# Attention and mixture-of-experts layer on one core: maximum ahead of the preceding weighted sum, other unit order, norm in portions, column sums folded by VectorE

## The chip, the core and the metric

The kernel runs on one core of a Trainium2 chip. The metric is the device time in microseconds (us) of one execution; lower is better. The engines are TensorE (PE, whose weight loads the profile lists as PEld), VectorE (DVE), ScalarE (ACT), GpSimd (POOL) and SyncE (SP), which here only issues DMAs. Each engine works through its own instructions strictly in order; semaphores hold an instruction until work of another engine is done, and everything behind it on that engine waits too.

## What is computed

Four sequences of 1024 rows of width 512 go through attention with 16 heads of 128, a norm over the rows, a router with 32 experts and a shared expert, and a second norm. All is float32. What matters here is the attention, cut from the reference:

```python
qkv = jnp.einsum('bsh,hf->bsf', x, w_qkv)
...
scores = jnp.einsum('bhqd,bhkd->bhqk', q, k) / jnp.sqrt(jnp.float32(D_HEAD))
probs = jax.nn.softmax(scores, axis=-1)
values = jnp.einsum('bhqk,bhkd->bhkd', probs, v)
...
out = jnp.einsum('bsf,fh->bsh', values, w_o)
...
x = _layernorm(x + _L0_attn_ref(x, L0_attn_w_qkv, L0_attn_w_o), axis=-1)
```

The einsum for `values` sums over the queries q. So a head needs no product of probabilities and values: it needs, for each key, the sum of the probabilities over all queries (a "column sum"), and multiplies v by it.

## The kernel before

There are 64 heads in all, M = 4 sequences x 16, taken two by two: pair i holds the even head 2i and the odd head 2i+1. A head has eight tiles t = 0 to 7 of 128 queries against 1024 keys. For each tile

- PE makes the scores in PSUM (`scores`, L2554: six matmuls of 128x512, since each float32 product is made as three products of rounded high and low parts). Two score tiles of two banks each take turns;
- DVE takes the row maximum (`max_tile`, L1885);
- ACT takes exp(score - maximum) and its row sum;
- DVE makes the reciprocal of the row sum (L1892) and adds the scaled tile to the head's column sums (`add_tile`, L1902 for tile 0 and L1905 for the others). This is called the weighted sum below.

The engines do the rest of the layer between these steps, at places that the functions `plain`, `first_half`, `second_half` and `last_half` of each engine write out by tile number. Nothing else sets the order.

**Early heads** (0 to 14, `plain`). ACT writes the exponentials to SBUF (`exp_tile` into `ex`, which is `rows_a`). Beside the scores, PE projects the next head's q, k and v (`project`, L2472, 72 matmuls) and, after the first two heads, makes four output tiles per head (`out_tile`, L2588, six matmuls each). POOL makes low parts (`lo_w`, `lo_wo`, `lo_cs`) and, for the late heads, sums of weight blocks: `sum_t` (L906 to L912) combines four blocks which SP has loaded (`load_t`), ACT rounds them (`hi_t_sums`), `lo_t` (L918) subtracts, and SP stores the result (`store_t`) in DRAM.

**Late heads** (15 to 63, `first_half` for an even head, `second_half` for an odd one). The projections of two heads are 21 `unit`s of six matmuls (L2485): seven for each head's q and k (P1 to P7), seven for both heads' v (V0 to V3 in the even half, three early ones in the odd half). ACT or DVE take the results out of PSUM (`evac_u` L1319, `evac_v` L1347, `add_block` L1935 and L1937, `lo_block` L1944). Here the exponentials stay in PSUM: `exp_here` (L1406) writes each tile over its scores, and `scores` for tile t+2 waits until the weighted sum of tile t is done (`dve_p`).

```python
on_pe.wait_ge(dve_p if banked and not (isinstance(n, int) and n == M - 1 and t >= 2) else act_e, n * T + t - 1)
```

**Column sums.** After a head's last tile, ACT copies the upper half of the column sums to `folded` (`upper_cs`), the lower half is added to it (`fold_cs`; DVE does it for early heads, L1920, and POOL for late ones, L939), ACT rounds it (`hi_cs`, L1376), POOL makes the low part (`lo_cs`, L899), and PE multiplies by ones to spread it over all partitions (`spread`, L2564, two matmuls, in tile 3 of the next head). DVE multiplies v by it (`times_v`, L1964).

**The norm** over a finished sequence's rows is done in the second pair of the next sequence (k == 1). ACT reads each of eight row tiles twice (`read_x`), POOL makes the factors (`scale_x`), and ACT writes four tiles in a row with them (`write_x`, L1175), twice.

## Time and profile before

| | |
|---|---|
| Median of 3 runs | 2806.37 us (2805.11 to 2806.81) |
| The profiled execution's own time | 2807.86 us |
| Its span, first to last instruction | 2806.3 us |
| PE busy | 2653.3 us, 95% |
| DVE busy | 2080.3 us, 74% |
| ACT busy | 1565.4 us, 56% |
| POOL busy | 1300.6 us, 46% |
| Mean granted TensorE clock | 0.988 |

The span and the execution's time differ by some 1.6 us that lie outside the first and last instruction. PE is the busiest engine. The attention takes about 2220 us of the span, and the experts and the last norm the rest. How much of the time PE loses has to be read from its waits and from the distances between its groups of matmuls, since a busy PE may still run slowly.

### The profile page before, as it was taken

The numbers are of one execution on the slowest core, as the hardware profiler recorded it, in microseconds if no ns is written. First come the engines' busy times: TensorE is split into PE (matmuls) and PEld (weight loads), VectorE is DVE, ScalarE is ACT, GpSimd is POOL, SyncE is SP. The second block draws the span as 40 slices with busy tenths as digits, with TensorE's granted clock in tenths as the row PEclk, the third lists the DMA queues.
The fourth block names the chain that finished last, engine by engine and source line by source line (L and its number), as shares of the span: only waits on it lengthen the run. The fifth ranks groups of instructions, "written<-read, shape, count | busy, mean of one in ns | idle before, by whom it ended". The sixth has DMA issues, their size and how long they took to land.

```text
span 2806.3 us, 40617 instructions
## 1 busy us (share of the span) xinstructions
PE 2653.3 (95%) x12450; PEld 2159.3 (77%) x12450; DVE 2080.3 (74%) x3096; ACT 1565.4 (56%) x2627; POOL 1300.6 (46%) x1042
## 2 busy tenths in 40 slices
PE   9888888999899999999999999899999999999998
PEld 7777777877777777777777777677777788788887
DVE  6877777888788888877888888788888787533346
ACT  5555555656665566576565556756656442244434
POOL 3666666635455454544444444444444220266520
PEclk9999999999999999999999999999999999999999
DMA  5454455544534336445333463533334231288954
GB/s 176 136 171 143 142 169 155 169 170 129 166 112 117 113 103 215 115 120 162 110 103 103 117 205 105 173 98 103 106 101 156 82 128 55 68 253 253 249 162 150
DMA packets 351134, 397.51 MB, mean 142 GB/s; under 512 B 132780, under 2 KB 269996, under 8 KB 350496
## 3 DMA queue, kind: packets, MB, share of 16 engines
q1 hardware_dynamic: 340512, 383.92, 44.2%
q0 software_dynamic: 10496, 12.02, 2.3%
q8 instruction: 66, 1.08, 0.2%
q14 instruction: 60, 0.49, 0.1%
HBM read 299.58 MB, written 106.43 MB: 145 GB/s over the span
## 4 chain that ended last, share of the span: by engine, by line
PE 48%; issue 20%; DVE 19%; ACT 7%; POOL 4%; DMA 1%; ACTq 1%; DVEq 0%; SPq 0%; POOLq 0%
PE banks L2485 11%; PE banks L2554 9%; DVE neg_max L1885 8%; PE banks L2588 6%; PE banks L2394 5%; PE banks L2443 5%; PE banks L2472 4%; PE banks L2456 3%; ACT banks L1406 2%; PE banks L2403 2%; DVE raws L1905 2%; DVE inv L1892 1%; DVE colsum L1905 1%; DVE y_sb L1976 1%; POOL w_all L887 1%
## 5 line engine op out<-in xcount | busy, mean ns | idle before, releaser
L2485 PE MATMUL banks<-xt,w_all 128*128 128x512 f32 x3024 | 764.4, 396 | 77.3 <-ACT rows_a L1319 34.1
L2554 PE MATMUL banks<-qk 128*128 128x512 f32 x3072 | 781.6, 390 | 2.3 <-DVE colsum L1905 1.4
L2485 PEld LDWEIGHTS banks<-xt,w_all 128*128 128x128 f32 x3024 | 563.4, 189 | 234.5 <-ACT rows_c L1347 50.2
L1406 ACT ACTIVATE banks<-banks,neg_max 128x1024 f32<-128x1024 f32 x384 | 417.4, 1087 | 526.7 <-DVE neg_max L1885 523.9
L1885 DVE TENSOR_REDUCE neg_max<-banks 128x1 f32<-128x1024 f32 x512 | 623.5, 1218 | 82.3 <-PE banks L2554 80.4
L2554 PEld LDWEIGHTS banks<-qk 128*128 128x128 f32 x3072 | 574.7, 188 | 128.0 <-DVE colsum L1905 4.3
L2588 PE MATMUL banks<-wo_sb,val 128*128 128x512 f32 x1536 | 380.2, 392 | 8.7 <-DVE y_sb L1976 7.0
L2588 PEld LDWEIGHTS banks<-wo_sb,val 128*128 128x128 f32 x1536 | 289.5, 189 | 73.4 <-DVE y_sb L1976 7.9
L2472 PE MATMUL banks<-xt,w_all 128*128 128x512 f32 x1152 | 287.8, 401 | 6.5 <-DVE xt L2105 6.5
L1892 DVE RECIPROCAL inv<-rowsum 128x1 f32<-128x1 f32 x512 | 82.3, 161 | 278.1 <-ACT banks L1406 274.1
L952 POOL TENSOR_TENSOR qk<-rows_a,qk 128x512 fp32r<-128x512 f32 x144 | 186.5, 1295 | 199.9 <-ACT qk L1331 199.9
L2472 PEld LDWEIGHTS banks<-xt,w_all 128*128 128x128 f32 x1152 | 225.0, 195 | 55.4 <-POOL w_all L887 6.5
L899 POOL TENSOR_TENSOR cs<-folded,cs 64x1024 fp32r<-64x1024 f32 x63 | 150.5, 2389 | 221.1 <-ACT cs L1376 221.1
L1398 ACT ACTIVATE rows_a<-banks,neg_max 128x1024 f32<-128x1024 f32 x128 | 143.1, 1118 | 166.6 <-DVE neg_max L1885 166.1
L1905 DVE SCALAR_TENSOR_TENSOR colsum<-banks,inv,colsum 128x1024 f32<-128x1024 f32 x168 | 215.7, 1284 | 7.2
L1905 DVE SCALAR_TENSOR_TENSOR raws<-banks,inv,raws 128x1024 f32<-128x1024 f32 x168 | 215.7, 1284 | 6.4 <-DVE inv L1892 0.6
L939 POOL TENSOR_TENSOR folded<-folded,colsum 64x1024 f32<-64x1024 f32 x24 | 57.5, 2395 | 314.0 <-ACT folded L1368 314.0
L2394 PE MATMUL banks<-xt 128*128 128x512 f32 x768 | 181.8, 392 | 0.9 <-DVE raws L1848 0.5
L1976 DVE TENSOR_TENSOR y_sb<-y_sb,banks 128x512 f32<-128x512 f32 x256 | 168.2, 679 | 14.5 <-PE banks L2588 12.5
L2394 PEld LDWEIGHTS banks<-xt 128*128 128x128 f32 x768 | 142.5, 188 | 31.0 <-issue 1.7
L1905 DVE SCALAR_TENSOR_TENSOR colsum<-rows_a,inv,colsum 128x1024 f32<-128x1024 f32 x105 | 160.6, 1530 | 4.2
L1078 POOL DMA_INDIRECT acc_rows<-rows_b,who x64 | 93.3, 1458 | 92.0 <-DMA acc_rows<-rows_b,who 42.7
(238 smaller groups left out, 3540.2 us busy)
## 6 DMA issues: line engine op xcount, KB each, us to landing
w_all<-w_jobs SPq DMA_DIRECT2D x144, 512.0 KB, 3.7
w_all<-w_jobs SPq DMA_DIRECT2D x72, 768.0 KB, 4.4
w_jobs<-xt SPq DMA_DIRECT2D x96, 256.0 KB, 3.2
x_jobs<-xt SPq DMA_DIRECT2D x48, 448.0 KB, 5.6
xt<-x_jobs SPq DMA_DIRECT2D x21, 1024.0 KB, 6.7
w_jobs<-w_all SPq DMA_DIRECT2D x72, 256.0 KB, 3.5
wo_raw<-in_w_o SPq DMA_DIRECT2D x63, 256.0 KB, 3.8
raws<-in_w_qkv SPq DMA_DIRECT2D x48, 256.0 KB, 4.3
```

Source lines behind the costliest of these rows:

```text
L899: pool.tensor_tensor(cs[0:HP], folded[:], rounded(cs[0:HP]), ALU.subtract).then_inc(pool_cs, 1)
L952: pool.tensor_tensor(to[:, LO], f32, rounded(to[:, HI]), ALU.subtract).then_inc(pool_ql, 1)
L1398: act.activation(ex[:, t % 2], p_s[:, t % 2], ACT.Exp, bias=neg_max[:, t % 2], accum_out=rowsum[:, t % 2]).then_inc(act_e, 1)
L1406: act.activation(p_s[:, t % 2], p_s[:, t % 2], ACT.Exp, bias=neg_max[:, t % 2], accum_out=rowsum[:, t % 2]).then_inc(act_e, 1)
L1885: dve.tensor_reduce(neg_max[:, t % 2], p_s[:, t % 2], AX_X, ALU.max, negate=True)\
L1905: dve.scalar_tensor_tensor(out=dst, in0=of[:, t % 2], scalar=inv[:, t % 2], in1=dst, op0=ALU.mult, op1=ALU.add).then_inc(dve_p, 1)
L1976: dve.tensor_tensor(y_sb[:, j], y_sb[:, j], p_o[:, j % 2], ALU.add).then_inc(dve_y, 1)
L2394: ins = pe.matmul(p_f(f % 2, r), s_gu[:, a, k, at], parts[:, PARTS_OF[u], b, k], start=(k == 0 and (a, b) == PASSES[0]), stop=(k == KC - 1 ...
L2472: ins = pe.matmul(p_g[:, g % 2], w_sb[:, a, r, c], xt[:, PLAIN_AT[half][c // 2], b, c % 2], start=(c == 0 and (a, b) == PASSES[0]), stop=( ...
L2485: ins = pe.matmul(psum[:, bank], w_slot[pos % 7][:, a, c], x[:, half, c], start=(opens and c == 0 and (a, half) == PASSES[0]), stop=(c == ...
L2554: ins = pe.matmul(p_s[:, t % 2, keys], qk[:, par, Q, a, at], qk[:, par, K, b, keys], start=((a, b) == PASSES[0]), stop=((a, b) == PASSES[-1]))
L2588: ins = pe.matmul(p_o[:, j % 2], val2[:, r, a, at], wo_sb[:, r, b], start=(r == 0 and (a, b) == PASSES[0]), stop=(r == 1 and (a, b) == PAS ...
```

## The change

Names and lines here are those of the kernel before, unless a row belongs to the kernel after.

1. Late heads write their exponentials to SBUF too, to `ex_late`, which is the whole of `raws` (the second set of column sums that lay there is gone; every head now uses `colsum`). `scores` waits for the exponential (`act_e`) alone.
2. On DVE, in late heads, the maximum of tile t stands ahead of the weighted sum of tile t-1.
3. The fold of late heads moves from POOL to DVE, into tile 1.
4. The units go in another order: P7 ahead of P6 and P4 ahead of P5, the second v unit ahead of P3, and the last early v unit behind an output tile. One ACT copy of a v unit becomes a DVE copy, `copy_v`, in tile 7 of an even head; the last v unit waits for it.
5. In early heads, POOL makes `lo_cs` ahead of `sum_t`; each head's second `lo_t` moves to the next head; `hi_t_sums` moves to tiles 5 and 0, `hi_x` to tile 6. SP stores and loads the head's own weights (`store_w`, `load_w`) ahead of `store_t` and `load_t`, and loads x earlier.
6. The norm's reads and writes go in portions of one or two tiles, each ahead of an exponential, over the tiles of the pair. Its reads use part of the x buffer as scratch, so SP's `load_x` of that pair waits for them.

```diff
-    unused_row = raws[:, 2 * NB:3 * NB]
+    ex_late = raws[:].rearrange("p (a s) -> p a s", a=2)
...
-    QK_UNITS, V_EARLY, V_MAIN = 7, (1, 3, 5), (0, 2, 4, 6)
+    QK_UNITS, V_EARLY, V_MAIN = 7, (1, 2, 4), (0, 3, 5, 6)
     RING_OF = (0, 0, 1, 1, 2, 2, 2)
-    P1, P2, P6, P7, P5, P4, P3 = range(7)
+    P1, P2, P7, P6, P4, P5, P3 = range(7)
...
         def plain(i, s):
             n = 2 * i + s
+            store_w(n + 1)
+            if n + 2 < H:
+                load_w(n + 2, n + 2)
             if 2 <= n - 1 <= H - 3:
                 store_t(n - 1, 1)
             if 2 <= n <= H - 3:
                 load_t(n, 0)
-            store_w(n + 1)
-            if n + 2 < H:
-                load_w(n + 2, n + 2)
...
-            if sums:
-                sum_t(n, 0)
+            late_sums = not isinstance(i, int) or 2 <= n - 1 <= H - 3
+            if late_sums:
+                lo_t(n - 1, 1)
             if not (is_first(i) and s == 0):
                 lo_cs(n - 1)
             if sums:
-                lo_t(n, 0)
+                sum_t(n, 0)
...
-            fold_cs(n - 1, 1)
             if at and b < B - 1:
                 sum_x(b, T * b)
             lo_cs(n - 1)
...
+                if t == 0 and (not isinstance(i, int) or 2 <= n - 1 <= H - 3):
+                    hi_t_sums(n - 1, 1)
+                if t == 5 and sums:
+                    hi_t_sums(n, 0)
...
                 if t == 0:
-                    upper_cs(n - 1, colsums[0])
+                    upper_cs(n - 1)
+                    if k1:
+                        read_x(c + 1, [2])
+                        write_x(c, [0, 1])
                 if t == 1:
+                    evac_u(i, AT_S1 + P1, m, 0)
                     if not (b == 0):
-                        evac_v(i, 6)
-                    evac_u(i, AT_S1 + P1, m, 0)
+                        evac_v(i, 5)
+                    if k1:
+                        read_x(c + 1, [3])
+                        write_x(c, [2, 3])
...
+        def copy_v(i):
+
+            on_dve.wait_ge(pe_u, units(i, AT_V + 2))
+            on_dve.wait_ge(dve_v, 2 * (2 * i))
+            dve.tensor_copy(v_sb[:, 1, NB:S], psum[:, 7]).then_inc(dve_ve, 1)
...
-                if t == 0:
-                    add_tile(b, n - 1, T - 1, colsums[1], p_s)
-                else:
-                    add_tile(b, n, t - 1, colsums[0], p_s)
                 if t == 2:
                     add_block(i, 0, m, 0)
+                if t == 5:
+                    add_block(i, 0, m, 2)
+                if t == 7:
+                    copy_v(i)
                 max_tile(n, t)
+                if t == 1:
+                    fold_cs(n - 1)
...
+                if t > 0:
+                    add_tile(n, t - 1, ex_late)
...
-            on_pe.wait_ge(dve_p if banked and not (isinstance(n, int) and n == M - 1 and t >= 2) else act_e, n * T + t - 1)
+            on_pe.wait_ge(act_e, n * T + t - 1)
...
-                for j in {0: (P1,), 1: (P2,), 2: (P6, P7), 3: (P5,), 4: (P4,), 5: (P3,)}.get(t, ()):
+                if t == 5:
+                    v_unit(b, i, 1)
+                for j in {0: (P1,), 1: (P2,), 2: (P7, P6), 3: (P4,), 4: (P5,), 5: (P3,)}.get(t, ()):
                     qk_unit(b, i, 0, j)
```

How POOL's order changes in an early even head, from its first `lo_wo` on. Before (L893 is `lo_wo`, L906 to L912 `sum_t`, L899 `lo_cs`, L918 `lo_t`, L887 `lo_w`):

```order
L893 TENSOR_TENSOR wo_sb<-wo_raw,wo_sb 128x512
L906 TENSOR_TENSOR rows_c<-rows_c 128x256
L908 TENSOR_TENSOR rows_c<-rows_c 128x256
L910 TENSOR_TENSOR rows_c<-rows_c 128x256
L912 TENSOR_TENSOR rows_c<-rows_c 128x256
L899 TENSOR_TENSOR cs<-folded,cs 64x1024
L918 TENSOR_TENSOR xt<-rows_c,xt 128x1024
L887 TENSOR_TENSOR w_all<-raws,w_all 128x512
L893 TENSOR_TENSOR wo_sb<-wo_raw,wo_sb 128x512
```

After (in the same roles L898, L904, L911 to L917, L892, L923). This is head 2, which has no `lo_t` of a head before it; from head 4 on one L923 stands between the first L898 and L904:

```order
L898 TENSOR_TENSOR wo_sb<-wo_raw,wo_sb 128x512
L904 TENSOR_TENSOR cs<-folded,cs 64x1024
L911 TENSOR_TENSOR rows_c<-rows_c 128x256
L913 TENSOR_TENSOR rows_c<-rows_c 128x256
L915 TENSOR_TENSOR rows_c<-rows_c 128x256
L917 TENSOR_TENSOR rows_c<-rows_c 128x256
L892 TENSOR_TENSOR w_all<-raws,w_all 128x512
L898 TENSOR_TENSOR wo_sb<-wo_raw,wo_sb 128x512
L923 TENSOR_TENSOR xt<-rows_c,xt 128x1024
```

The low part of the column sums stood behind four operations that wait for SP's load of weight blocks; it now stands ahead of them, and `lo_t` stands behind a second `lo_wo`.

How DVE's order changes from tile 6 of a late even head to tile 2 of the odd head behind it. Before (L1885 maximum, L1944 `lo_block`, L1892 and L1905 or L1902 weighted sum, L1937 `add_block`):

```order
L1885 TENSOR_REDUCE neg_max<-banks 128x1
L1944 TENSOR_TENSOR qk<-banks,qk 128x512
L1892 RECIPROCAL inv<-rowsum 128x1
L1905 SCALAR_TENSOR_TENSOR raws<-banks,inv,raws 128x1024
L1885 TENSOR_REDUCE neg_max<-banks 128x1
L1892 RECIPROCAL inv<-rowsum 128x1
L1905 SCALAR_TENSOR_TENSOR raws<-banks,inv,raws 128x1024
L1885 TENSOR_REDUCE neg_max<-banks 128x1
L1892 RECIPROCAL inv<-rowsum 128x1
L1902 TENSOR_SCALAR colsum<-banks,inv 128x1024
L1885 TENSOR_REDUCE neg_max<-banks 128x1
L1937 SCALAR_TENSOR_TENSOR rows_a<-banks,rows_a 128x512
```

After (L1884 maximum, L1937 `lo_block`, L1891 and L1898 or L1895 weighted sum, L2005 `copy_v`, L1913 fold, L1930 `add_block`):

```order
L1884 TENSOR_REDUCE neg_max<-banks 128x1
L1937 TENSOR_TENSOR qk<-banks,qk 128x512
L1891 RECIPROCAL inv<-rowsum 128x1
L1898 SCALAR_TENSOR_TENSOR colsum<-raws,inv,colsum 128x1024
L2005 COPY v_sb<-banks 128x512
L1884 TENSOR_REDUCE neg_max<-banks 128x1
L1891 RECIPROCAL inv<-rowsum 128x1
L1898 SCALAR_TENSOR_TENSOR colsum<-raws,inv,colsum 128x1024
L1891 RECIPROCAL inv<-rowsum 128x1
L1898 SCALAR_TENSOR_TENSOR colsum<-raws,inv,colsum 128x1024
L1884 TENSOR_REDUCE neg_max<-banks 128x1 x2
L1913 TENSOR_TENSOR folded<-folded,colsum 64x1024
```

The maxima now stand ahead of the weighted sums that they stood behind, except at tile 0; the weighted sums read `raws` in SBUF instead of the banks; the copy of a v unit and the fold are new in this queue.

## Rows read from the trace of the kernel before

**Rows 1.** PE's waits over the span: total us, times, longest.

```profile
PE banks L2564 <- POOL cs L899: 40.8, 6, 7.6
PE banks L2485 <- ACT rows_a L1319: 34.1, 29, 1.8
PE banks L2485 <- ACT rows_c L1347: 30.3, 40, 3.9
PE banks L2588 <- DVE y_sb L1976: 7.0, 6, 1.3
```

**Rows 2.** Two stages: length, then busy PE, PEld, DVE, ACT, POOL; clock, DMA.

```profile
65.80:521.40 455.60, 407.82 (x1729) 332.30 (x1729) 365.15 (x429) 255.79 (x391) 290.90 (x204) 0.95 0.52 155
621.90:2164.50 1542.60, 1468.23 (x6304) 1179.40 (x6303) 1228.70 (x1565) 958.49 (x1596) 737.81 (x565) 0.99 0.42 127
```

**Rows 3.** Timeline of PE: start us, us; spreads of early heads.

```profile
331.51 1.22 PE L2564 MATMUL banks<-cs,ones 128*128 128x512 f32 x2 [6.88 <-POOL cs L899]
...
521.42 0.62 PE L2564 MATMUL banks<-cs,ones 128*128 128x512 f32 x2
...
554.52 0.62 PE L2564 MATMUL banks<-cs,ones 128*128 128x512 f32 x2
```

**Rows 4.** Timeline of PE just behind the spread at 331.51.

```profile
332.52 4.10 PE L2472 MATMUL banks<-xt,w_all 128*128 128x512 f32 x12
```

**Rows 5.** Timeline of POOL in the same even head.

```profile
317.63 1.29 POOL L893 TENSOR_TENSOR wo_sb<-wo_raw,wo_sb 128x512 fp32r<-128x512 f32 x1 [3.45 <-ACT wo_sb L1289]
325.80 0.72 POOL L906 TENSOR_TENSOR rows_c<-rows_c 128x256 f32<-128x256 f32 x1 [6.87 <-DMA rows_c<-in_w_qkv]
...
328.88 2.34 POOL L899 TENSOR_TENSOR cs<-folded,cs 64x1024 fp32r<-64x1024 f32 x1
```

**Rows 6.** Timelines of SP's queue and of ACT in that head.

```profile
325.35 2.59 SPq L536 DMA_DIRECT2D raws<-in_w_qkv  x3
...
320.11 1.05 ACT L1376 CAST cs<-folded 64x1024 fp32r<-64x1024 f32 x1 [1.15 <-DVE folded L1920]
...
329.87 0.62 ACT L1282 CAST w_all<-raws 128x512 fp32r<-128x512 f32 x1 [4.50 <-DMA raws<-in_w_qkv]
```

**Rows 7.** Timeline of PE over one late pair of heads.

```profile
994.74 0.61 PE L2564 MATMUL banks<-cs,ones 128*128 128x512 f32 x2
...
1050.84 3.06 PE L2485 MATMUL banks<-xt,w_all 128*128 128x512 f32 x12 [1.25 <-ACT rows_a L1319]
...
1060.54 0.61 PE L2564 MATMUL banks<-cs,ones 128*128 128x512 f32 x2
```

**Rows 8.** Timelines of PE and ACT, pair with the norm.

```profile
688.09 0.61 PE L2564 MATMUL banks<-cs,ones 128*128 128x512 f32 x2
...
740.94 2.71 PE L2485 MATMUL banks<-xt,w_all 128*128 128x512 f32 x6 [3.31 <-ACT rows_c L1347]
...
764.43 0.62 PE L2564 MATMUL banks<-cs,ones 128*128 128x512 f32 x2
...
737.50 2.92 ACT L1175 ACTIVATE y_sb<-y_sb,n_shift,n_scale 128x512 f32<-128x512 f32 x4
```

**Rows 9.** The page's part 5: busy us, mean ns, idle before.

```profile
L1885 DVE TENSOR_REDUCE neg_max<-banks 128x1 f32<-128x1024 f32 x512 | 623.5, 1218 | 82.3 <-PE banks L2554 80.4
...
L1892 DVE RECIPROCAL inv<-rowsum 128x1 f32<-128x1 f32 x512 | 82.3, 161 | 278.1 <-ACT banks L1406 274.1
...
L1905 DVE SCALAR_TENSOR_TENSOR colsum<-banks,inv,colsum 128x1024 f32<-128x1024 f32 x168 | 215.7, 1284 | 7.2
...
L1905 DVE SCALAR_TENSOR_TENSOR colsum<-rows_a,inv,colsum 128x1024 f32<-128x1024 f32 x105 | 160.6, 1530 | 4.2
```

**Rows 10.** Views of lines 1905 and 1920: ns min/median/max.

```profile
L1905 DVE SCALAR_TENSOR_TENSOR colsum<-rows_a,inv,colsum x105: 1283/1354/2926, 36.7 to 2214.9; 128x1024 f32<-128x1024 f32 x105
...
L1920 DVE TENSOR_TENSOR folded<-folded,colsum x14: 1205/1207/1765, 60.7 to 548.3; 64x1024 f32<-64x1024 f32 x14
```

**Rows 11.** Groups by line: a 128x512 read of PSUM on DVE.

```profile
L1944 DVE TENSOR_TENSOR qk<-banks,qk 128x512 fp32r<-128x512 f32 x48 | 32.7, 682 | 0.0
```

More of the change, by code:

```diff
@@ L688, in first_half @@
                 load_block(b, i, 5)
+                load_block(b, i, 4)
+            if end and more:
                 load_block(b, i, 6)
@@ L698, in second_half @@
             last = b == B - 1 and not x_too
[L699 removed]
+            if x_too and not k1:
                 load_x(b, k + 1, T * b + k + 1)
```

284 lines of the change are left out of this document (136 added, 148 removed).

## The prediction

> **What bounds the kernel now.** I read PE's waits first [rows 1], then the two long stages of the attention by windows [rows 2], then the distances between PE's spreads, one per head, on its timeline [rows 3, 7, 8]. PE is the engine to watch: it is busy for 408 of 456 us in the early stage and 1468 of 1543 us in the late one [rows 2]. But its busy time hides how fast it runs, so I measure by distance. The undisturbed early head from 521.42 to 554.52 takes 33.10 us [rows 3] for 146 matmuls of 128x512 (48 for scores, 72 for the projections, 24 for outputs, 2 for the spread): 0.227 us each. That is the floor.
>
> *Early stage.* Twelve heads lie between the spreads at 65.8 and 521.4, in 455.6 us [rows 2]. Eleven cost at least 33.1 us, the first, without output tiles, 122 x 0.227 = 27.7 us: 391.8 us. The excess is 63.8 us. Of it 40.8 us are six waits of a spread for POOL's low part, and 7.0 us six waits for an add to `y_sb` [rows 1]. The rest is mostly the clock: the granted clock over the stage is 0.95 [rows 2], and behind such a wait 12 matmuls last 4.10 us [rows 4], where 12 x 0.227 plus the tail of one, 0.16, is 2.88.
>
> *Late stage.* From 621.9 to 2164.5 there are 23 pairs in 1542.6 us [rows 2]. A pair has 274 matmuls (96 scores, 126 in units, 48 outputs, 4 in spreads), so 62.1 us at least. One takes 65.8 us [rows 7]. A pair with the norm takes 76.3 us [rows 8], and I take that for all three. The other twenty share 1542.6 - 228.9 = 1313.7 us: 65.7 each, an excess of 3.6, 72 us in all. The waits behind it are for ACT's copies of units [rows 1], such as the 1.25 us at 1050.84 [rows 7]: ACT is in order, the copy stands behind an exponential, that waits for a maximum, and on DVE the maximum stands behind the weighted sum of the tile before, which waits for an exponential in turn. DVE stood still for 274 us ahead of its reciprocals for that reason [rows 9].
>
> **The change, part by part.**
>
> *Early heads.* In the even head shown, PE was free for the spread at 331.51 - 6.88 = 324.6 [rows 3]. POOL's `lo_cs` began at 328.88, behind a `sum_t` that waited 6.87 us for SP's load of blocks; yet ACT had its input ready at 320.11 + 1.05 = 321.2 [rows 5, 6]. In the new order POOL makes `lo_wo` to 318.9, the late `lo_t` (about as long as `lo_cs`, 2.34), so to 321.3, then `lo_cs` to 323.6 [rows 5]. The spread is ready about 1 us early. Something else is late next: ACT waited until 329.87 for the weights that SP issued only at 325.35 [rows 6], and an exponential stands behind that. `store_w` and `load_w` now go ahead of `store_t` and `load_t`, so this wait goes too; the price is that the blocks land later. They feed `sum_t`, `hi_t_sums` and `lo_t`, now at tiles 5 and 0, where ACT may wait some 3 us in an odd head. PE needs tile t's exponential only for tile t+2, two tiles of 4.1 us later, so most of that is covered; without the cover it is about 3 us per two heads. I leave 3.0 us per two heads (the `y_sb` wait of 1.2, the rest for the spread and these loads), 18 of 63.8: gain 46 us. Bounds: 20 us, if the spread still waits 3 to 4 us each time and the clock falls with it, and 60 us, if nothing waits. Moving `load_x` and `hi_x` up costs nothing: POOL and SP reach `store_x_step` no later than about 2 us after the old time, and it feeds DRAM alone.
>
> *Exponentials to SBUF, maximum first.* PE's tile t+2 is freed one weighted sum earlier, and exponentials start right behind scores. That alone could give back the whole 3.6 us of a pair. Against it stands new work on DVE: two folds of 1.2 us [rows 10], one `copy_v` like a 128x512 read of PSUM, 0.7 us [rows 11], and weighted sums that now read two operands from SBUF. These take 1.284 us from the banks but 1.530 on average from `rows_a` in the early heads, where POOL is busy 64% of the time [rows 2, 9]; the longest took 2.93 us against a least of 1.28 [rows 10]. So the stretch is between 0 and 1.6 us each. POOL is 48% busy in the late stage and loses the folds, so I take at most the early mean, 0.25 us. DVE per pair: 1228.7 / 23 = 53.4 now [rows 2], + 2.4 + 0.7 + 16 x 0.25 = 60.5 us, against PE's 62.1. DVE does not set the pace by its sum, but it has little slack at single places.
>
> The Trainium skill, SBUF — State Buffer, section Who interferes with whom, speaks against this part: a DVE instruction with two SBUF inputs and a GpSimd instruction that reads SBUF exclude each other for a whole instruction. The trace agrees in kind: a sum over banks is never stretched, one over `rows_a` is [rows 9, 10].
>
> Two places where it pays. First, `copy_v`. It stands behind the weighted sum of tile 5, and the last v unit waits for it. From the start of tile 6's scores: 1.5 us to their end, then the maximum 1.22, `lo_block` 0.68, reciprocal 0.16, sum 1.28 to 1.53, copy 0.68 [rows 9, 11]: 5.5 to 5.8 us. PE gets to the unit after three groups of six, 4.1 us. A new wait of 1.4 to 1.7 us per pair. Second, the third `add_block` of an odd head stands behind a sum that falls together with POOL's `lo_cs` (2.3 us): P3 waits 0.3 to 1.0. Together 1.7 to 2.7 us in place of 3.6; the old waits for `evac_u` go, since P7 now fills the 1.36 us in which P6 waited 1.25 [rows 7]. I take 2.6: gain 1.0 x 20 = 20 us. Bounds: a loss of 1 us and a gain of 3 us per pair.
>
> *Norm in portions.* The four writes in a row are 2.92 us on ACT, and the wait of 3.31 us on PE came with them [rows 8]. Portions of two halve the block, 1.5 us. The eight reads and eight writes remain, ahead of exponentials and unit copies, and POOL's `scale_x` now stands ahead of the next head's `lo_val`. SP's `load_x`, and POOL's `sum_x` behind it, wait for the reads; a tile of x is needed only at the end of the sequence, so nothing of PE waits for it. Of the 76.3 - 62.1 = 14.2 us I take 5 back, between 0 and 9: 15 us in three pairs.
>
> *The rest* (entry into the late stage, last head, experts) keeps its order nearly: 0, give or take 3 us.
>
> Sum: 46 + 20 + 15 = 81 us off the span of 2806.3 us: 2725 us. The profiled execution took 1.6 us more than its span, 2807.9, which is 1.5 above the median of 2806.4; against the median the forecast is 2726 us.
>
> **Rivals.**
>
> *DVE becomes the bound of the late stage.* For it: DVE would be 97% busy. Against it: fewer POOL instructions than in early heads. POOL works 32.1 us per pair [rows 2], less two folds of 2.3 to 2.4 some 27.4, 44% of the time; if each of 16 sums meets it that often and waits 1 us, the mean stretch is 0.44 us and DVE's sum is 63.5 us, and with 3 us of waits for PE a pair takes 66.5: the late stage loses 0.8 x 20 = 16 us. Time: 2806 - 46 - 12 + 16 = 2764 us. The Trainium skill's rule (SBUF — State Buffer, Who interferes with whom), taken as it stands, leads to this case.
>
> *The early wait only changes its cause.* The spread waits for `lo_t` or `lo_wo`, which wait for ACT and SP. For it: `lo_t` is a new member ahead of `lo_cs`. Against it: the times above. Each keeps more than half, gain 20: 2752 us; with a late stage unchanged as well, 2771 us.
>
> *The late waits nearly vanish.* If `copy_v` and the fold fit, a pair takes 63.5 us, gain 2.2 x 20 = 44, 24 in the norm pairs, 50 early: 2688 us.
>
> *Slower.* One mechanism: sums and POOL exclude each other so often that DVE sets a longer pace everywhere late. The early and norm gains, 61 us over 23 pairs, are used up when a pair takes 65.7 + 2.7 = 68.4 us, so from a DVE sum of about 66 us, a mean stretch of 0.6 us; at 0.8 us it is 2806 - 61 + 23 x 6 = 2883 us. The worst single row shows 1.6 us, the mean 0.25.
>
> **How the numbers follow.** Forecast (2700 to 2750) 0.58; DVE the bound 0.17; early wait stays 0.10; late waits vanish 0.10; slower 0.05. The range from 2680 to 2775 us takes in the first four but for the outer part of each. A measurement of this kernel tells about 0.2% (5.6 us) from no change. Faster 0.94, same 0.01, slower 0.05.
>
> **What would show it.** The six waits for POOL's `cs` gone or under 1 us, and the clock at 1.00 in early heads. A new wait of PE for DVE's `v_sb` of about 1.5 us, once a pair, 24 times. The weighted sums from `raws` at 1.4 to 1.6 us; above 1.8 the DVE rival is right. DVE's idle time ahead of reciprocals down from 274 us to under 60. Pairs at 64 to 65.5 us, with the norm at 71. If early heads still take over 36 us, or the norm pairs over 74, the prediction is wrong there.

## The result, and the profile after

The changed kernel takes 2781.6 us, the median of 4 runs (2778.7 to 2784.0), against 2805.8 for the kernel before on the same chip: a ratio of 0.9913, 95% interval 0.9896 to 0.9930. The profiled execution has a span of 2781.6 us. The change saves 24 us. The forecast was 80 us, and the time lies above 2775 us, the upper end of its range. The direction was right and the size wrong.

PE's waits in the changed kernel, as engine, tile, line, releaser, then the total in us, how often, and the longest, answer to [rows 1]:

```profile
PE banks L2490 <- DVE v_sb L2005: 49.5, 24, 2.9
PE banks L2571 <- POOL cs L904: 12.9, 5, 2.8
PE banks L2490 <- DVE rows_a L1928: 12.1, 24, 1.2
PE banks L2561 <- POOL qk L953: 11.6, 3, 4.0
```

The six waits for POOL's low part of the column sums have become five of 2.3 to 2.8 us. There is the wait for `copy_v` that was forecast, 24 times, but 2.1 us long. And there are three waits of 4.0 us in the norm pairs that I had not named.

The two stages by windows (length, then busy time of PE, weight loads, DVE, ACT and POOL, granted clock) answer to [rows 2]:

```profile
66.92:499.60 432.68, 406.92 (x1730) 330.49 (x1729) 387.45 (x429) 254.97 (x390) 291.40 (x200) 0.97 0.54 161
599.90:2137.70 1537.80, 1463.62 (x6303) 1191.37 (x6302) 1346.85 (x1633) 948.30 (x1571) 736.53 (x519) 0.99 0.42 128
```

The early stage gave 22.9 us (455.6 to 432.7) and the 23 late pairs gave 4.8 (1542.6 to 1537.8). DVE rose to 1346.9 us, 58.6 per pair; I had put it at 60.5, with 16 longer sums. But only 14 of the 16 read two operands: the sum of tile 0 reads one, and got shorter, 0.75 us from `raws` where it took 1.28 from the banks. POOL lost its folds and yet works 736.5 us, where it worked 737.8 [rows 2]. That is the first sign of what went wrong. It shows in the groups of operations, with busy time and mean ns of one behind the bar, and behind the next bar the engine's idle time ahead of them. First the kernel before, then the changed one; [rows 9] has the sums before, 1284 ns over banks and 1530 over `rows_a`:

```profile
L943 POOL TENSOR_TENSOR val<-rows_b,val 128x1024 fp32r<-128x1024 f32 x48 | 115.1, 2397 | 21.6 <-ACT val L1389 21.6
L959 POOL TENSOR_TENSOR v_sb<-v_sb,rows_c 128x512 f32<-128x512 f32 x48 | 61.8, 1287 | 0.0
```

```profile
L944 POOL TENSOR_TENSOR val<-rows_b,val 128x1024 fp32r<-128x1024 f32 x48 | 140.6, 2929 | 23.8 <-ACT val L1390 23.8
L962 POOL TENSOR_TENSOR v_sb<-v_sb,rows_c 128x512 f32<-128x512 f32 x48 | 102.6, 2138 | 0.0
L1898 DVE SCALAR_TENSOR_TENSOR colsum<-raws,inv,colsum 128x1024 f32<-128x1024 f32 x343 | 538.4, 1570 | 13.5
L1898 DVE SCALAR_TENSOR_TENSOR colsum<-rows_a,inv,colsum 128x1024 f32<-128x1024 f32 x105 | 177.7, 1692 | 4.2
L1884 DVE TENSOR_REDUCE neg_max<-banks 128x1 f32<-128x1024 f32 x512 | 624.3, 1220 | 227.7 <-PE banks L2561 225.9
```

The last row also answers a sign that I had named. DVE no longer stands still ahead of its reciprocals, where it lost 274 us, but it stands 228 us ahead of its maxima, where it lost 82 [rows 9]: more than half of that idle time only has another place.

The mean stretch of a sum, 0.29 us, is almost what I took (0.25). But POOL's operations are stretched too, an add to `v_sb` by 0.85 us, and the stretch is not spread evenly. DVE's timeline in a late pair (start, duration), from tile 6 of the even head on:

```profile
820.11 0.68 DVE L1937 TENSOR_TENSOR qk<-banks,qk 128x512 fp32r<-128x512 f32 x1
820.71 0.15 DVE L1891 RECIPROCAL inv<-rowsum 128x1 f32<-128x1 f32 x1
820.89 2.20 DVE L1898 SCALAR_TENSOR_TENSOR colsum<-raws,inv,colsum 128x1024 f32<-128x1024 f32 x1
823.02 0.68 DVE L2005 COPY v_sb<-banks 128x512 f32<-128x512 f32 x1
823.62 1.21 DVE L1884 TENSOR_REDUCE neg_max<-banks 128x1 f32<-128x1024 f32 x1
824.75 0.15 DVE L1891 RECIPROCAL inv<-rowsum 128x1 f32<-128x1 f32 x1
824.94 1.62 DVE L1898 SCALAR_TENSOR_TENSOR colsum<-raws,inv,colsum 128x1024 f32<-128x1024 f32 x1
826.48 0.15 DVE L1891 RECIPROCAL inv<-rowsum 128x1 f32<-128x1 f32 x1
826.67 2.11 DVE L1898 SCALAR_TENSOR_TENSOR colsum<-raws,inv,colsum 128x1024 f32<-128x1024 f32 x1
```

POOL and PE in the same stretch:

```profile
820.74 1.27 POOL L953 TENSOR_TENSOR qk<-rows_a,qk 128x512 fp32r<-128x512 f32 x1
821.98 2.25 POOL L962 TENSOR_TENSOR v_sb<-v_sb,rows_c 128x512 f32<-128x512 f32 x1
824.19 1.29 POOL L898 TENSOR_TENSOR wo_sb<-wo_raw,wo_sb 128x512 fp32r<-128x512 f32 x1
825.44 2.26 POOL L962 TENSOR_TENSOR v_sb<-v_sb,rows_c 128x512 f32<-128x512 f32 x1
```

```profile
823.75 1.85 PE L2490 MATMUL banks<-xt,w_all 128*128 128x512 f32 x6 [2.11 <-DVE v_sb L2005]
825.41 2.76 PE L2561 MATMUL banks<-qk 128*128 128x512 f32 x6
```

The two engines take turns. The sum that begins at 820.89 finds POOL's block under way and ends 1.08 us after it (823.09 and 822.01); POOL's add, begun at 821.98, ends 1.14 us after the sum (824.23). The sums at 824.94 and 826.67 repeat it: each ends 1.08 us after the POOL operation that it found. This agrees with the Trainium skill, SBUF — State Buffer, Who interferes with whom: one of the two holds what both need as an exclusive lock, and the other waits until it is done.

I follow the stages by the distances between PE's spreads on its timeline; all are first start to first start, in us. "Early" is 12 heads, "late" 23 pairs, "norm" the mean of the three pairs with the norm, "other" the mean of the remaining twenty. The kernels of the experiments are told below.

| kernel | ratio to before | early | late | norm | other |
|---|---|---|---|---|---|
| before | 1 | 455.6 | 1542.6 | 76.0 | 65.7 |
| changed | 0.9913 | 432.7 | 1537.8 | 73.0 | 65.9 |
| a1 `copy_v` first | 0.9880 | 431.7 | 1530.8 | 72.7 | 65.6 |
| a2 `lo_cs` first | 0.9997 | 452.7 | 1539.4 | 73.0 | 66.0 |
| a3 `scale_x` later | 0.9862 | 433.0 | 1531.4 | 71.4 | 65.9 |
| a4 before + early part | 0.9925 | 430.9 | 1542.6 | 76.0 | 65.7 |
| b1 `lo_t` first | 0.9871 | 423.5 | 1539.7 | 73.0 | 66.0 |
| b2 less POOL late | 0.9754 | 433.9 | 1498.7 | 70.3 | 64.4 |
| b3 late exponentials in banks | 1.0907 | 433.6 | 1802.9 | 78.1 | 78.4 |
| b4 four moves | 0.9803 | 424.3 | 1518.2 | 70.9 | 65.3 |
| c1 b4 + two moves | 0.9769 | 426.5 | 1512.4 | 71.2 | 64.9 |
| c2 b4, less POOL late | 0.9627 | 424.6 | 1473.6 | 70.9 | 63.0 |
| c3 changed, small fold | 0.9871 | 427.8 | 1534.2 | 73.0 | 65.8 |
| c4 b4 + early move | 0.9797 | 427.1 | 1520.2 | 71.2 | 65.3 |
| d1 c4, less POOL early | 0.9706 | 398.6 | 1520.5 | 71.3 | 65.3 |
| d2 b4 + late move | 0.9770 | 424.6 | 1512.5 | 71.1 | 65.0 |

The 95% intervals of the ratios are 0.0013 to 0.0018 to either side, that of a2 0.0009. The stages are from one profile of each kernel. Kernels with the same early orders differ by up to 3 us in the early stage (430.9 to 433.9 and 423.5 to 424.6). In the late stage of the changed kernel an odd distance is 33.5 us at full clock and 35.1 where the clock falls, so two pairs more or less with a fall make 3.2 us.

### The profile page after: what moved, and what is told of

The parts are those of the page before. It is cut to its first block, busy times and chain, and to the rows that moved or that the text cites. A ratio compares the mean times of both kernels' runs of the same rounds, so it can differ in the third digit from the quotient of the medians.

```text
span 2781.6 us, 40677 instructions
## 1 busy us (share of the span) xinstructions
PE 2654.2 (95%) x12450; PEld 2177.2 (78%) x12450; DVE 2227.8 (80%) x3169; ACT 1555.7 (56%) x2603; POOL 1305.8 (47%) x993
## 3 DMA queue, kind: packets, MB, share of 16 engines
q8 instruction: 66, 1.08, 0.2%
## 4 chain that ended last, share of the span: by engine, by line
PE 66%; issue 4%; DVE 3%; POOL 1%; ACT 1%; DVEq 0%; ACTq 0%; POOLq 0%
PE banks L2490 21%; PE banks L2561 15%; PE banks L2595 9%; PE banks L2399 6%; PE banks L2448 5%; PE banks L2461 3%; PE banks L2408 3%; PE banks L2323 1%; PE banks L2571 1%; PE banks L2435 1%; DVE rows_a L1928 1%; DVE qk L1937 1%; DVE v_sb L2005 1%; PE banks L2347 0%; DVE colsum L1898 0%
## 5 line engine op out<-in xcount | busy, mean ns | idle before, releaser
L2490 PE MATMUL banks<-xt,w_all 128*128 128x512 f32 x3024 | 759.8, 395 | 65.9 <-DVE v_sb L2005 49.5
L1884 DVE TENSOR_REDUCE neg_max<-banks 128x1 f32<-128x1024 f32 x512 | 624.3, 1220 | 227.7 <-PE banks L2561 225.9
L2561 PE MATMUL banks<-qk 128*128 128x512 f32 x3072 | 791.0, 393 | 12.3 <-POOL qk L953 11.6
L1398 ACT ACTIVATE raws<-banks,neg_max 128x1024 f32<-128x1024 f32 x392 | 437.7, 1117 | 490.7 <-DVE neg_max L1884 487.2
L2561 PEld LDWEIGHTS banks<-qk 128*128 128x128 f32 x3072 | 583.9, 190 | 137.2 <-POOL qk L953 12.9
L1898 DVE SCALAR_TENSOR_TENSOR colsum<-raws,inv,colsum 128x1024 f32<-128x1024 f32 x343 | 538.4, 1570 | 13.5
L904 POOL TENSOR_TENSOR cs<-folded,cs 64x1024 fp32r<-64x1024 f32 x63 | 157.1, 2494 | 639.1 <-ACT cs L1377 639.1
L953 POOL TENSOR_TENSOR qk<-rows_a,qk 128x512 fp32r<-128x512 f32 x144 | 204.2, 1425 | 132.2 <-ACT qk L1335 132.2
L1398 ACT ACTIVATE rows_a<-banks,neg_max 128x1024 f32<-128x1024 f32 x120 | 133.9, 1116 | 133.4 <-DVE neg_max L1884 132.7
L1898 DVE SCALAR_TENSOR_TENSOR colsum<-rows_a,inv,colsum 128x1024 f32<-128x1024 f32 x105 | 177.7, 1692 | 4.2
L944 POOL TENSOR_TENSOR val<-rows_b,val 128x1024 fp32r<-128x1024 f32 x48 | 140.6, 2929 | 23.8 <-ACT val L1390 23.8
L1372 ACT COPY folded<-colsum 64x1024 f32<-64x1024 f32 x63 | 66.0, 1047 | 139.6 <-DVE colsum L1898 139.2
L898 POOL TENSOR_TENSOR wo_sb<-wo_raw,wo_sb 128x512 fp32r<-128x512 f32 x63 | 96.1, 1525 | 49.0 <-ACT wo_sb L1293 49.0
```

Source lines behind the costliest of these rows:

```text
L904: pool.tensor_tensor(cs[0:HP], folded[:], rounded(cs[0:HP]), ALU.subtract).then_inc(pool_cs, 1)
L944: pool.tensor_tensor(val2[:, r, LO], val[:, r], rounded(val2[:, r, HI]), ALU.subtract)\
L953: pool.tensor_tensor(to[:, LO], f32, rounded(to[:, HI]), ALU.subtract).then_inc(pool_ql, 1)
L1398: act.activation(to[:, t % 2], p_s[:, t % 2], ACT.Exp, bias=neg_max[:, t % 2], accum_out=rowsum[:, t % 2]).then_inc(act_e, 1)
L1884: dve.tensor_reduce(neg_max[:, t % 2], p_s[:, t % 2], AX_X, ALU.max, negate=True)\
L1898: dve.scalar_tensor_tensor(out=colsum[:], in0=of[:, t % 2], scalar=inv[:, t % 2], in1=colsum[:], op0=ALU.mult, op1=ALU.add).then_inc(dve_p, 1)
```

## The experiments

**a1: `copy_v` ahead of the sum of tile 5.**

```diff
@@ DVE, first_half
-                if t == 7:
-                    copy_v(i)
                 max_tile(n, t)
...
                 if t == 6:
                     lo_block(m, 1)
+                    copy_v(i)
                 if t > 0:
                     add_tile(n, t - 1, ex_late)
```

> The changed kernel with one move: copy_v stands ahead of the weighted sum of tile 5, not behind it. Theory (the one wait of 2.1 us per pair, and the low clock behind it, is what took the late gain): PE's wait for v_sb goes in 24 pairs, 24 x 2.1 = 50 us, and with it some of the clock drops (about 6 x 1.6 us); the late stage takes 1480 to 1495 us instead of 1538, the kernel 2722 to 2740 us. Rival 1 (DVE is the bound, 1347 us busy of 1538): the sum of tile 5 now ends 0.7 us later, the next wait takes the place of this one, and less than 15 us come back: 2766 to 2781 us. Rival 2 (half of it): the wait goes, but the third add_block or a copy of ACT is late instead by about 1 us per pair: 2745 to 2755 us.

Measured: 0.9880, interval 0.9864 to 0.9895. The late stage takes 1530.8 us, 7 less. PE's wait for `v_sb` is gone, and in its place stands, in the first row of its waits and on ACT's timeline:

```profile
PE banks L2489 <- ACT rows_a L1323: 33.7, 20, 1.9
```

```profile
890.04 1.05 ACT L1372 COPY folded<-colsum 64x1024 f32<-64x1024 f32 x1 [3.38 <-DVE colsum L1898]
891.25 1.11 ACT L1398 ACTIVATE raws<-banks,neg_max 128x1024 f32<-128x1024 f32 x1 [0.17 <-DVE neg_max L1884]
892.26 0.19 ACT L1398 ACTIVATION_READ_ACCUMULATOR raws<-banks,neg_max 128x1 f32 x1
892.36 0.59 ACT L1323 ACTIVATE rows_a<-banks 128x512 f32<-128x512 f32 x1
```

The copy of the odd head's first unit stands behind an exponential, whose maximum stands behind the last two sums of the even head, 2.2 us each. DVE's lag was only passed on. An ordinary pair at full clock still takes 65.2 to 65.3 us, as in the changed kernel; what a1 gave is a milder fall of the clock in the others (odd distances of 34.7 in place of 35.1) and 0.2 us in each norm pair. The amount is that of rival 1, the place to which the wait moved is one that rival 2 named, and my theory of the single wait is wrong.

**a2: `lo_cs` ahead of the late `lo_t`. b1: `lo_t` ahead of `lo_wo`.** Both try to bring the spread in time in the even early heads; b1 was made after a2.

```diff
@@ POOL, plain: a2
+            if not (is_first(i) and s == 0):
+                lo_cs(n - 1)
             if late_sums:
                 lo_t(n - 1, 1)
-            if not (is_first(i) and s == 0):
-                lo_cs(n - 1)
@@ POOL, plain: b1
+            if late_sums:
+                lo_t(n - 1, 1)
             if s == 0 and not is_first(i):
                 lo_wo(n - 2, 0)
-            if late_sums:
-                lo_t(n - 1, 1)
```

> The changed kernel with one move: in the early heads POOL makes the low part of the column sums (lo_cs) ahead of the late lo_t. Theory (three operations in a row on POOL, each stretched, make the spread 2.6 us late in the even heads, and the low clock behind it costs as much again): POOL makes lo_cs at about 310.7 to 313.5 in the head shown, PE is free at 314.3, the wait of 2.3 to 2.8 us goes in five even heads and four to five odd ones' waits stay as they are. Gain 5 x 2.6 for the wait and 5 x 2 for the clock = 15 to 25 us in the early stage (432.7 us now, then 408 to 418). Rival (lo_t is late instead, and holds sum_t and the loads behind it, or the y_sb wait takes over): less than 6 us.

> The changed kernel with one move: in the even early heads POOL makes the late lo_t ahead of lo_wo, not behind it. In the profile of the changed kernel POOL stood still for 3.46 us ahead of lo_wo at 308.44, and lo_t's input had been ready since 302.8. Theory (the chain on POOL of three stretched operations is what makes the spread late; making lo_cs earlier by holding up lo_t cost more, since lo_t releases the next loads): lo_t runs in that gap, lo_cs begins at 310.7 instead of 313.5, the spread waits under 0.5 us in five even heads and the clock stays up: early stage 410 to 420 us instead of 432.7, kernel 2762 to 2770 us. Rival (ACT's exponentials are late anyway in these heads, and take the wait's place): less than 6 us, 2776 or more.

a2 measured 0.9997 (0.9988 to 1.0006): the whole gain of the change is lost, and the early stage takes 452.7 us. The waits for `cs` fall to 4.5 us in all, but `lo_t`, now later, releases the next load of blocks. ACT waits 7.05 us for the sums of that load, with the exponentials in line behind it, and PE waits for these:

```profile
PE banks L2561 <- ACT rows_a L1398: 19.3, 16, 2.2
```

```profile
315.29 1.05 ACT L1298 CAST xt<-rows_c 128x1024 fp32r<-128x1024 f32 x1 [7.05 <-POOL rows_c L917]
316.24 1.11 ACT L1398 ACTIVATE rows_a<-banks,neg_max 128x1024 f32<-128x1024 f32 x1
```

b1 measured 0.9871 (0.9854 to 0.9887). `lo_t` runs in a gap of POOL, one spread waits in place of five, and the odd loop heads reach 33.1 us, the floor of [rows 3], mostly. But the even ones stay at 38.2 to 38.6. Their wait has moved to the out tiles. The early stage takes 423.5 us, between theory (410 to 420) and rival:

```profile
PE banks L2595 <- POOL wo_sb L898: 17.7, 6, 3.4
```

**a3: `scale_x` behind the third low block.**

```diff
@@ POOL, first_half
             add_v(i, 0)
-            if k1:
-                scale_x(2 * (b - 1))
             lo_val(n - 1, 1)
...
             lo_block(m, 1, 2)
+            if k1:
+                scale_x(2 * (b - 1))
             add_v(i, 1)
```

> The changed kernel with one move: in the three norm pairs POOL's scale_x of the first portion goes behind the third low block, instead of ahead of lo_val. Theory (scale_x is 4 us on POOL and PE's wait of 4.0 us for the low block of qk is its direct cost): three waits of 4.0 us and the low clock behind them go, 12 to 16 us: norm pairs 69 us instead of 73.05, kernel 2766 to 2770 us. Rival (the block is late because ACT's reads of the norm stand ahead of its copies, POOL only ends last): PE waits for ACT's qk or unit copies instead, under 4 us gained: 2778 us or more.

Measured: 0.9862 (0.9847 to 0.9877). The three waits of 4.0 us are gone, three of up to 1.9 us for ACT's copy follow, and a norm pair takes 71.4 us in place of 73.0, 5 us in all, less than half of what theory said. The time of 2770.1 us stands at the edge of the theory's range all the same. The ratio speaks for 14 us, the spans of the profiles for 8, the late stage for 6.4; I claim 5 to 6 for the move, since it touches no other stage; where the rest lies is open.

**a4: the kernel before with the early orders alone.** The edit is the part of the diff that lies in `plain` of SP, POOL and ACT, with the late stage as it was.

```diff
@@ kernel before, ACT, plain
-                if t in (3, 6) and sums:
-                    hi_t_sums(n, t // 6)
-                if t == 7 and (s == 1 or is_first(i)):
+                if t == 0 and (not isinstance(i, int) or 2 <= n - 1 <= H - 3):
+                    hi_t_sums(n - 1, 1)
+                if t == 5 and sums:
+                    hi_t_sums(n, 0)
+                if t == 6 and more and (s == 1 or is_first(i)):
                     hi_x(0, i + s)
```

> The kernel before with the early part of the change alone: the orders of SP, POOL and ACT in the heads of the first stage, nothing in the late stage. Theory (the parts add, since the stages follow one another): the early stage takes 431 to 435 us instead of 455.6 as it does in the changed kernel, the rest stays as before: 2781 to 2785 us. Since the changed kernel has 2781.6, this leaves nothing or 2 us for all the rest of the change (late pairs and norm +15, end of the kernel and start -3, rest). More exactly from the windows: 2806.3 - 22.9 = 2783. Rival (the early gain needs the exponentials of the last early heads or the fold elsewhere): early stage above 440 us, 2790 or more.

Measured: 0.9925 (0.9911 to 0.9938). Early 430.9 us, the late stage as before to 0.1 us, 4 us more between them. So the early orders are nearly the whole gain of the change: 20 of its 24 us.

**b2: less work for POOL in the late stage. c2: the same on b4.** `lo_val`, `lo_block` and `add_v` work on 8 of their 512 or 1024 columns, so most of this work is left out.

```diff
@@ POOL, lo_val, lo_block, add_v (one of three)
+            w = slice(0, 8)
-            pool.tensor_tensor(to, to, term, ALU.add).then_inc(pool_va, 1)
+            pool.tensor_tensor(to[:, w], to[:, w], term[:, w], ALU.add).then_inc(pool_va, 1)
```

> The changed kernel, but POOL's operations lo_val, lo_block and add_v of the late stage work on 8 columns only (most of that work is left out). Theory (DVE's weighted sums are stretched because POOL reads SBUF at the same time, and this makes copy_v and the sums behind it late): the sums from raws take 1.28 to 1.35 us instead of 1.57 on average, the wait for v_sb falls from 2.1 to about 1.2 us, the third add_block's wait goes, the half intervals of 33.5 become 32.0 to 32.4, low-clock stretches go from the late stage, the norm pairs lose about 2 us each; kernel 2735 to 2755 us. Rival (the order on DVE is what makes it late, and the stretch is small or comes from ACT or DMA): sums stay above 1.5 us, gain under 10 us.

> The kernel with four moves (b4), with POOL's lo_val, lo_block and add_v of the late stage on 8 columns only (most of that work left out). On the changed kernel the same cut was worth 42 us, of which I put about half down to waits and half down to the low clock and the norm pairs. Theory (once copy_v is in time, the stretch is mostly covered): the cut is worth 15 to 25 us here, P3's wait 1.18 to 0.6 us, copies of units 0.8 to 0.3: 2727 to 2737 us. Rival (DVE's total is what counts, so the cut is worth the same again): 2705 to 2715 us.

b2 measured 0.9754 (0.9737 to 0.9770): 42 us less than the changed kernel, 39 of them in the late stage. The order of DVE is the same, only the sums are shorter, and the wait for `v_sb` falls from 2.1 to 1.2 us. A pair at full clock takes 64.4 us in place of 65.3, which is that 0.9 us, and no ordinary pair shows a fall of the clock any more. In ordinary late pairs PE waited for no result of POOL's, in either kernel, so it is DVE's sums through which the cut acts there; in the norm pairs, 2.7 us each, POOL's own time goes too. One part of the theory missed: PE's wait for the third block stays (11.8 us, 23 times).

```profile
L1901 DVE SCALAR_TENSOR_TENSOR colsum<-raws,inv,colsum 128x1024 f32<-128x1024 f32 x343 | 459.4, 1339 | 13.5
```

```profile
PE banks L2493 <- DVE v_sb L2008: 28.8, 24, 1.3
```

c2 measured 0.9627 (0.9611 to 0.9643), 2702.6 us, 49 less than b4. The theory is wrong, and the rival's amount (2705 to 2715) is even passed by 2 us. Its reason, DVE's total, is not shown by that: see c3. In the late stage the four kernels make a square: changed 1537.8, moves alone 1518.2, cut alone 1498.7, both 1473.6. The cut is worth 39 us without the moves and 45 with them.

**b3: late exponentials in place in the banks**, as in the kernel before, with every other part of the change kept.

```diff
@@ ACT, first_half and second_half
-                exp_tile(n, t, ex_late)
+                exp_tile(n, t, p_s)
@@ DVE, first_half and second_half
-                    add_tile(n, t - 1, ex_late)
+                    add_tile(n, t - 1, p_s)
@@ PE, scores
-            on_pe.wait_ge(act_e, n * T + t - 1)
+            on_pe.wait_ge(dve_p if banked and not (isinstance(n, int) and n == M - 1 and t >= 2) else act_e, n * T + t - 1)
```

> The changed kernel, but the exponentials of the late stage stay in their PSUM banks as in the kernel before (order of DVE, units, folds as changed). PE's scores of tile t+2 then wait for the weighted sum of tile t instead of its exponential, and the sums read only one operand from SBUF. Theory (leaving the banks early is worth more than what the stretched sums cost): sums take 1.28 us, but PE waits at scores for DVE's sums, pairs 67 to 71 us instead of 65.3: kernel 2820 to 2900 us. Rival (with the maximum first DVE has enough slack that the banks are free in time anyway, and the stretch is the larger item): V3's wait under 1.3 us, 2755 to 2775 us.

Measured: 1.0907 (1.0889 to 1.0925), a late pair 78.4 us. PE waits 219 us for the weighted sums of tiles 1 to 7, 173 times, and 43 us for those of tile 0, 25 times. So with the maximum first the exponentials have to leave the banks. The other half, exponentials in SBUF with the old order on DVE, was not run. The same profile is the control for the stretch. With one SBUF operand less, the stretch of these groups is gone in the late stage, on both engines, though POOL has the same work:

```profile
L1898 DVE SCALAR_TENSOR_TENSOR colsum<-banks,inv,colsum 128x1024 f32<-128x1024 f32 x336 | 431.3, 1284 | 13.3
L944 POOL TENSOR_TENSOR val<-rows_b,val 128x1024 fp32r<-128x1024 f32 x48 | 114.6, 2387 | 25.9 <-ACT val L1390 25.9
L962 POOL TENSOR_TENSOR v_sb<-v_sb,rows_c 128x512 f32<-128x512 f32 x48 | 61.7, 1286 | 0.8 <-DVE v_sb L2005 0.8
```

**b4: four moves.** a1, a3 and b1 together, and ACT's copy that a1 exposed, one exponential earlier:

```diff
@@ ACT, second_half
                 if t == 0:
                     upper_cs(n - 1)
+                    evac_u(i, AT_S1 + P1, m, 0)
...
                 if t == 1:
-                    evac_u(i, AT_S1 + P1, m, 0)
```

> The changed kernel with four moves together: copy_v ahead of the sum of tile 5; scale_x behind the third low block; lo_t ahead of lo_wo in the early heads; and ACT's copy of the first unit of the odd head ahead of the exponential of its tile 0, since PE waited 1.94 us for that copy once copy_v was no longer late. Theory (each wait is a place, and they add): early -15 to -20 us, norm -11, late pairs 65.3 to about 63.9 with fewer low-clock stretches, -25 to -35; 2715 to 2730 us. Rival (DVE is the bound between tile 6 of the even head and tile 1 of the odd one, where it works without a pause for 15 us): the wait only moves on once more, late pairs stay at 65.2, 2748 to 2756 us.

Measured: 0.9803 (0.9787 to 0.9820), 2751.8 us. It is faster than both kernels, but by the rival's amount (2748 to 2756). A pair at full clock takes 33.4 + 31.8 = 65.2 us, as the rival had it; the third `add_block`'s wait grew from 0.45 to 1.18. What the late moves bring lies in the norm pairs and in the clock: no ordinary pair but two is longer than 65.2.

**c3: the fold on 8 columns**, on the changed kernel (most of DVE's fold left out).

```diff
@@ DVE, fold_cs
-            dve.tensor_tensor(folded[:], folded[:], colsum[0:HP], ALU.add).then_inc(dve_cs, 1)
+            w = slice(0, 8)
+            dve.tensor_tensor(folded[:, w], folded[:, w], colsum[0:HP, w], ALU.add).then_inc(dve_cs, 1)
```

> The changed kernel with DVE's fold of the column sums on 8 columns only (most of the fold left out, in all heads but the last). Theory (DVE is short of time at places, not in sum; the fold stands behind the places where PE waits): 0 to 10 us in the whole kernel, the v_sb wait stays at 2.1 us. Rival (DVE is the bound in sum): 1.1 us per head, 48 to 60 us: 2722 to 2735 us.

Measured: 0.9871 (0.9854 to 0.9887), 10 us less than the changed kernel by the medians and 12 by the ratios, at the upper end of the theory: 4.9 in the early stage, 3.6 in the late one. PE waits 49.7 us for `v_sb`, as without the cut. 46 folds of 1.2 us, 55 us of DVE's work, were taken out in the late stage and worth 3.6 us there. Of these, 3.2 are two pairs less with a fall of the clock; a pair at full clock takes 65.3 us as before. So DVE is not the late stage's bound in sum.

**c1, c4, d2: the next waits.** c4 is b4 with an early move, d2 is b4 with a late one, c1 has both.

```diff
@@ POOL, plain: c4, c1
+            if s == 0 and not is_first(i):
+                lo_wo(n - 1, 1)
             if not end:
                 lo_w(n + 2, Q)
...
-            if s == 0 and not is_first(i):
-                lo_wo(n - 1, 1)
@@ DVE, second_half: d2, c1
-                if t == 3:
-                    add_block(i, AT_S1, m, 2)
...
                 if t == 2:
                     add_block(i, AT_S1, m, 1)
+                    add_block(i, AT_S1, m, 2)
```

> The kernel with four moves (b4) and two more: in the even early heads POOL makes the second lo_wo ahead of the low part of the q weights (PE waited 3.3 us for it once the spread was in time), and in the odd late heads DVE makes the third add_block ahead of the weighted sum of tile 1, not behind it. Theory (both remaining waits are places in the order): the wait for wo_sb falls from 3.3 to about 1.1 us in six heads, 12 to 18 us with the clock; P3's wait of 1.18 us goes in about 20 pairs, 20 to 24 us: 2710 to 2722 us. Rival (DVE has no slack there; the sum pushed back makes the maximum of tile 3 and the spread late): the gain is the early one alone, 2736 to 2742 us.

> The kernel with four moves (b4) and the early one of the two further moves alone: the second lo_wo ahead of the low part of the q weights in the even early heads. Theory: early stage 424 to about 408 us, kernel 2734 to 2740 us. Rival (the q weights, 2.3 us later, hold up SP's next load and with it ACT's exponentials): under 5 us, 2747 or more.

> The kernel with four moves (b4) and the third add_block of the odd late heads ahead of the sum of tile 1, without the early move of the second lo_wo, which was worth nothing by itself. Theory (the parts add): 2743 to 2747 us, a pair 64.3 us. Rival (the early move was what helped in that run): 2750 us or more.

c4 measured 0.9797 (0.9781 to 0.9814), 2752.2 us: no gain over b4, as the rival said, though its reason (SP's next load held up) is not shown. The waits for `wo_sb` went but for one of 1.2 us, waits for `val` (7.1 us, 5 times) and `y_sb` (11.6, 9 times) came. c1 measured 0.9769 (0.9753 to 0.9786), 2745.0 us, above both of its ranges: the early move gave nothing and the late one 7 us. d2 measured 0.9770 (0.9752 to 0.9788): 2744.3 us, the best whole kernel here, though not apart from c1, and inside the theory's range. The wait of 1.18 us for the third block is gone, and one of 0.7 us in the even half (`rows_b`, 15.2 us, 21 times) takes half of it back. A pair at full clock has 64.4 us, as the theory of d2 said; over all twenty it is 65.0.

**d1: less work for POOL in the early loop heads**, on c4: `lo_w`, `sum_t` and `lo_t` on a few columns (most of it left out).

```diff
@@ POOL, lo_t (one of three)
+            w = slice(0, S) if isinstance(n, int) else slice(0, 8)
-            pool.tensor_tensor(low, t_own, rounded(high), ALU.subtract).then_inc(pool_tw, 1)
+            pool.tensor_tensor(low[:, w], t_own[:, w], rounded(high[:, w]), ALU.subtract).then_inc(pool_tw, 1)
```

> The kernel with four moves and the second lo_wo ahead of the q weights (c4), with POOL's lo_w, sum_t and lo_t of the ten loop heads of the early stage on a few columns only (most of that work left out; 30 us of POOL's work per two heads). Theory (in the early stage too DVE is late because its sums from rows_a are stretched beside POOL, 1.6 to 1.7 us instead of 1.28): sums from rows_a under 1.45 us, the waits for val and y_sb (1.6 and 1.8 us) go to under 0.5 us, even loop heads 34 to 35 us instead of 37.5, early stage 427 to 410 us. Rival (the loads from DRAM and ACT's place in line set it): even heads stay above 36.5 us although the sums are short.

Measured: 0.9706 (0.9690 to 0.9722). The early stage takes 398.6 us in place of 427.1 in c4, and from the fifth distance between spreads on every head takes 33.1 us, even ones too. The window of the stage, with the clock at 1.00, and the group of sums:

```profile
65.44:464.00 398.56, 393.79 (x1729) 323.68 (x1728) 352.79 (x429) 254.22 (x390) 147.14 (x202) 1.00 0.59 177
```

```profile
L1901 DVE SCALAR_TENSOR_TENSOR colsum<-rows_a,inv,colsum 128x1024 f32<-128x1024 f32 x105 | 149.9, 1427 | 4.2
```

SP issues the same loads in the same order as in c4, and so does ACT with its operations, so neither holds the even heads by itself. But SP's loads wait in part for buffers that POOL frees, so they can also come earlier here. The cut takes away three things: POOL's own time, the stretch of DVE's sums (1680 ns in c4, 1427 here), and this hold on the loads. How much each is worth in the early stage is not told apart.

## Why the prediction was wrong

*Early heads: 46 us forecast, 22.9 measured.* The step that failed is "`lo_wo` to 318.9, the late `lo_t` (about as long as `lo_cs`, 2.34), so to 321.3, then `lo_cs` to 323.6 [rows 5]. The spread is ready about 1 us early." The order of events was right, the durations were not:

```profile
308.44 2.28 POOL L898 TENSOR_TENSOR wo_sb<-wo_raw,wo_sb 128x512 fp32r<-128x512 f32 x1 [3.46 <-ACT wo_sb L1293]
310.68 2.86 POOL L923 TENSOR_TENSOR xt<-rows_c,xt 128x1024 fp32r<-128x1024 f32 x1
313.49 3.34 POOL L904 TENSOR_TENSOR cs<-folded,cs 64x1024 fp32r<-64x1024 f32 x1
```

The three take 8.4 us, where I had 1.3 + 2.3 + 2.3. The same three operations have a DVE operation on SBUF beside each of them, and each ends 1.1 to 2.3 us behind the end of that one (309.57, 311.27 and 314.62):

```profile
308.36 1.21 DVE L1913 TENSOR_TENSOR folded<-folded,colsum 64x1024 f32<-64x1024 f32 x1
309.67 1.60 DVE L1895 TENSOR_SCALAR colsum<-rows_a,inv 128x1024 f32<-128x1024 f32 x1
313.11 1.51 DVE L1898 SCALAR_TENSOR_TENSOR colsum<-rows_a,inv,colsum 128x1024 f32<-128x1024 f32 x1
```

The 2.34 us that I had taken for `lo_cs` come from a place in the kernel before (328.88 to 331.22) where DVE stood still:

```profile
332.33 1.29 DVE L1964 TENSOR_TENSOR rows_b<-v_sb,banks 128x512 f32<-128x512 f32 x2 [5.85 <-PE banks L2564]
```

PE was free at 314.5 and waited 2.59 us; its next 12 matmuls lasted 5.32 us in place of 2.88. That is the worst of the five: behind the others they lasted 3.80, 4.49, 3.92 and 2.90 us, 6.0 us too much over all five, and with the waits of 12.9 us that makes 19 us, where the forecast left at most 11 (18 less 1.2 for each of six `y_sb` waits). Other late results of POOL and DVE that the forecast did not have came with it: three waits for `wo_sb` (4.6 us, and 2.6 for the low clock behind the longest of them) and two for `val` (2.7 us). Together that is 18 of the 23 us that are missing; the rest is spread over small waits. I had let POOL stretch DVE's sums and not asked what DVE does to POOL. The wait for SP's load did go, as forecast. That is the 22.9 us. With POOL cut the early stage reached 398.6 us (d1), 57 less than before: the room that I saw was there, but not with POOL's work in it. b1 took four of the five waits of the spread away with all work in place, and they were worth 9 us of the stage, since `wo_sb` was late next.

*Ordinary late pairs: 20 us gain forecast, 4 us loss measured.* 65.73 became 65.95. Of the terms, the new waits fit in sum: 2.11 for `v_sb` (I had 1.4 to 1.7, with a sum of at most 1.53 us where 2.20 stand at 820.89) and 0.45 for the third block (0.3 to 1.0), 2.56 together where I took 2.6. That the sum fits is partly luck: the first is above its range, the second near its lower end. Two things were missing. The floor of 62.1 us is too low: a pair at full clock has 65.3, less 2.56 is 62.7, part of it the 0.13 us by which the first group behind each wait is longer (1.65 for 1.52). And the clock: behind the 2.1 us wait it stayed up in most pairs and fell in six of twenty, whose odd distance is 35.1 in place of 33.5, some 10 us over the stage. I had written no clock term for the late stage, though [rows 4] showed me one in the early stage. The mean stretch was right. What failed is its use as a mean over 16 sums: in DVE's unbroken run from tile 6 of the even head on three of them carry 0.9, 0.3 and 0.8 us. That is why a1 moved the wait and b2 shortened it.

*DVE as the bound.* Not in sum (c3), but it sets the pace over that run, so the truth (65.95) lies between my forecast (64.7) and the first rival (66.5 us a pair). Taking the forecast's one wait away (a1) gave 7 us where 24 x 2.1 = 50 us had stood in PE's waits, and each later move was partly taken back.

*Norm pairs: 5 us each forecast, 3.1 measured* (76.0 to 73.0). The term that was too large is the 5 us itself: I named `scale_x` ahead of `lo_val` and gave it no price. PE waited 3.98 us for it at the odd head's first scores; a3 got 1.6 us a pair back.

*The rest* was near 0: the entry to the late stage takes 100.3 us (100.4 before), the start 1.1 us more, the end 2.1 us more.
